# Delta over 64 rows in alternating partition halves; the weight's second half quantised in two 512-column chunks; M's third tile ahead of x G's fourth

## What is computed

```
delta = lora_B @ lora_A * 32/64                   # rank 64, 512 x 512
idx   = searchsorted(thresholds, (weight + delta) / exp(scale_log), side='left')   # 8 levels, 7 cuts
w_eff = codebook[idx] * exp(scale_log) + delta    # by groups of 128 columns
q, k, v = split((x @ w_eff.T) @ Wqkv + bqkv)
x = x + softmax(q k.T / sqrt(128)) v @ Wo + bo
y = x @ W.T + 2 * sum_e gate_e * (x A_e.T) B_e.T  # gates: softmax of the two best of 8 logits
x = x + y @ (scale * (qweight - zero_point)).T + bias
```

## Time and profile before

| | |
|---|---|
| device time, median of 3 runs | 107.92 us (107.66 to 108.25) |
| device time of the profiled execution | 108.04 us |
| span of its profile | 106.2 us |
| TensorE (PE) busy | 101.5 us, 96% |
| VectorE (DVE) busy | 66.3 us, 62% |
| ScalarE (ACT) busy | 51.9 us, 49% |
| GpSimd (POOL) busy | 34.3 us, 32% |
| mean granted TensorE clock | 0.997 |

### The profile page before, as it was taken

One profiled execution on the slowest core, in us unless ns is written; L12 is line 12 of the kernel. 1 busy time (PEld: TensorE's weight loads), 2 busy tenths in 40 slices (PEclk: granted clock), 3 DMA queues, 4 the chain that ended last, 5 costly groups with the idle time before them and its releaser, 6 DMA issues.

```text
span 106.2 us, 1428 instructions
## 1 busy us (share of the span) xinstructions
PE 101.5 (96%) x505; PEld 83.6 (79%) x505; DVE 66.3 (62%) x157; ACT 51.9 (49%) x92; POOL 34.3 (32%) x34
## 2 busy tenths in 40 slices
PE   6899999999999999999999999999999999999980
PEld 6734588889777899899888787889898888888850
DVE  1196799999999899325999653014946802572440
ACT  4038789999999954734222238272038204002000
POOL 3000063799919993696000056400000400000000
PEclk9999999999999999999999999999999999999998
DMA  1999999960000000000000000000000540000072
GB/s 38 323 259 396 408 402 406 408 244 0 3 0 0 0 0 0 9 0 0 0 0 0 0 0 0 0 6 0 0 0 0 225 170 0 6 0 0 0 294 104
DMA packets 4455, 9.83 MB, mean 93 GB/s; under 512 B 736, under 2 KB 736, under 8 KB 4448
## 3 DMA queue, kind: packets, MB, share of 16 engines
q1 hardware_dynamic: 4304, 9.48, 24.3%
q10 hardware_dynamic: 144, 0.26, 0.8%
HBM read 7.64 MB, written 2.10 MB: 92 GB/s over the span
## 4 chain that ended last, share of the span: by engine, by line
PE 89%; DMA 4%; DVE 3%; ACT 1%; issue 0%
PE psum L860 19%; PE psum L862 19%; PE psum L861 19%; PE psum L884 7%; PE psum L876 4%; DMA lora<-in_lora 4%; PE psum L895 3%; PE psum L910 3%; PE psum L901 3%; PE psum L905 3%; PE psum L1011 2%; PE psum L1032 2%; PE psum L1026 2%; ACT moe L459 1%; PE psum L1018 1%; PE psum L928 1%
## 5 line engine op out<-in xcount | busy, mean ns | idle before, releaser
L665 DVE COPY_PREDICATED cond_work<-cond_work,psum 128x1024 f32<-128x1024 int32 x10 | 13.7, 1374 | 1.3 <-ACT cond_work L359 0.9
L860 PE MATMUL psum<-G_hi,xT_hi 128*128 128x512 f32 x32 | 12.9, 402 | 0.0
L861 PE MATMUL psum<-G_lo,xT_hi 128*128 128x512 f32 x32 | 12.5, 391 | 0.0
L862 PE MATMUL psum<-G_hi,xT_lo 128*128 128x512 f32 x32 | 12.5, 390 | 0.0
L578 POOL TENSOR_TENSOR hl<-hl,hl_bias 128x272 f32<-128x272 f32 (+2 forms) x4 | 3.1, 774 | 27.0 <-ACT hl L370 14.3
L359 ACT ACTIVATE cond_work<-cond_n,cut_bias 128x1024 f32<-128x1024 f32 x10 | 11.4, 1158 | 0.7 <-DVE cond_n L704 0.7
L520 POOL TENSOR_TENSOR xT_lo<-xT,xT_hi 128x1024 fp32r<-128x1024 f32 x4 | 9.6, 2402 | 2.4 <-DVE cond_work L671 2.4
L860 PE MATMUL psum<-xT_hi,split_b_hi 128*128 128x512 f32 x24 | 9.7, 402 | 0.0
L862 PE MATMUL psum<-xT_hi,split_b_lo 128*128 128x512 f32 x24 | 9.4, 391 | 0.0
L861 PE MATMUL psum<-xT_lo,split_b_hi 128*128 128x512 f32 x24 | 9.4, 390 | 0.0
L520 POOL TENSOR_TENSOR split_a_lo<-moe,split_a_hi 128x512 fp32r<-128x512 f32 x3 | 4.3, 1436 | 15.0 <-ACT split_a_hi L336 12.5
(11 more groups left out here) (168 smaller groups left out, 239.8 us busy)
## 6 DMA issues: line engine op xcount, KB each, us to landing
out<-cond_work SPq DMA_DIRECT2D x8, 256.0 KB, 2.1
q_i<-in_q_t SPq DMA_DIRECT2D x4, 256.0 KB, 7.5
moe<-in_moe_w SPq DMA_DIRECT2D x4, 256.0 KB, 7.5
cond_n<-in_cond_w SPq DMA_DIRECT2D x2, 512.0 KB, 7.1
xT<-in_x_t SPq DMA_DIRECT2D x2, 512.0 KB, 8.2
xT<-in_x_t SPq DMA_DIRECT2D x1, 1024.0 KB, 12.7
wqkv_n<-in_wqkv SPq DMA_DIRECT2D x1, 768.0 KB, 10.7
hlT<-in_hl_t SPq DMA_DIRECT2D x1, 272.0 KB, 6.7
```

What stands on the lines that cost most here:

```text
L665: dve.copy_predicated(by_group(half(level, h)), by_group(beyond[n % len(beyond)].bitcast(I32)), psum[EARLY][:, at:at + GROUPS // 2].unsque ...
L860: pe.matmul(out_ap, l_hi, r_hi, start=first, stop=False)
L861: pe.matmul(out_ap, l_hi, r_lo, start=False, stop=False)
L862: return pe.matmul(out_ap, l_lo, r_hi, start=False, stop=last)
```

## The change

The diff has seven parts.

- Delta: each product takes 64 of the 128 partitions, the lower half for o = 0, 2 and the upper for o = 1, 3; the scale is no longer halved.
- `w_full(0)` moves ahead of VectorE's last small operations on the cuts.
- The rounding of moe tile 1 moves from ScalarE to GpSimd, with a semaphore of its own.
- `CHUNKS`: the quantisation runs in three chunks: tiles 0 and 1 (1024 columns), tile 2, tile 3 (512 columns each). 21 masks and picks take the place of 14. VectorE's and ScalarE's lists are laid out anew from the second chunk on.
- PE: the four `M_part(2, i)` come before `y_x(3)`, only the four `M_part(3, i)` behind it.
- PE: `y_o(0)` comes ahead of `scores(1, 0)`.
- The last result is added and stored in two column halves.

```diff
-    LORA_COPIES = 2
-    LORA_SCALE = 32.0 / 64.0 / LORA_COPIES
+    LORA_SCALE = 32.0 / 64.0
+    CHUNKS = (slice(0, 2), slice(2, 3), slice(3, 4))
...
-            for b in range(BATCH):
+            for b in range(BATCH - 1):
                 sp.wait_ge(y_ready, b + 1)
                 sp.dma_start(out[b], y_out[:, b, :]).then_inc(stored, 16)
+            b = BATCH - 1
+            for n in range(2):
+                sp.wait_ge(y_ready, b + n + 1)
+                s = slice(n * C // 2, (n + 1) * C // 2)
+                sp.dma_start(out[b, :, s], y_out[:, b, s]).then_inc(stored, 16)
...
             beyond_cut(0, 0)
-            moe_hi(1)
             w_hi(1)
...
             beyond_cut(0, 1)
+            beyond_cut(1, 1)
             hl_raw(1, 5)
-            beyond_cut(1, 1)
+            beyond_cut(2, 1)
...
             hl_raw(2, 6, HL)
-            beyond_cut(2, 1)
             x_hi(1)
...
             w_eff_hi(1)
             beyond_cut(3, 1)
+            beyond_cut(4, 1)
+            beyond_cut(5, 1)
             wqkv_round(1)
-            beyond_cut(4, 1)
+            beyond_cut(6, 1)
+            beyond_cut(0, 2)
+            beyond_cut(1, 2)
             wqkv_round(2)
+            beyond_cut(2, 2)
+            w_eff_hi(2)
             wqkv_round(3)
-            beyond_cut(5, 1)
-            beyond_cut(6, 1)
+            for j in range(3, CUTS):
+                beyond_cut(j, 2)
             act.wait_ge(loaded["woT"], 16)
             rounded(woT_hi, woT[:, :, :], woT_hi_ready)
-            w_eff_hi(2)
             w_eff_hi(3)
...
+            pool.wait_ge(loaded["moe1"], 16)
+            pool.tensor_copy(split_a_hi[:, 1, :], moe[:, 1, :]).then_inc(moe_first_hi_ready, 1)
             moe_rest(1)
...
+            w_full(0)
             dve.wait_ge(dve_step, cuts_at)
             keep(1, ALU.min, 3)
...
             for i in range(CT):
                 G_rest(i)
-            pick(0, 1)
-            pick(1, 1)
+            for j in range(3):
+                pick(j, 1)
             w_eff(0)
             w_eff(1)
...
-            pick(2, 1)
-            pick(3, 1)
-            pick(4, 1)
-            pick(5, 1)
-            pick(6, 1)
+            for j in range(3, CUTS):
+                pick(j, 1)
+            pick(0, 2)
             w_eff(2)
+            pick(1, 2)
+            w_eff_lo(2)
+            for j in range(2, CUTS):
+                pick(j, 2)
             w_eff(3)
-            w_eff_lo(2)
             w_eff_lo(3)
...
             for o in range(CT):
-                pe.matmul(psum[DELTA_BANKS[o]][:, :], lora[:, 0, o * P:(o + 1) * P], lora[:, 1, :], start=True, stop=True)\
+                rows = slice(o % 2 * RANK, (o % 2 + 1) * RANK)
+                pe.matmul(psum[DELTA_BANKS[o]][:, :], lora[rows, 0, o * P:(o + 1) * P], lora[rows, 1, :],
+                          start=True, stop=True)\
                   .then_inc(delta_done, 1)
...
-            pe.wait_ge(picked, HALVES * CUTS)
+            pe.wait_ge(wqkv_ready, 3)
+            pe.wait_ge(w_eff_late_lo_ready, 1)
+            for i in range(CT):
+                M_part(2, i)
+            pe.wait_ge(picked, len(CHUNKS) * CUTS)
             y_x(3)
             pe.wait_ge(wqkv_ready, CT)
+            pe.wait_ge(w_eff_late_lo_ready, 2)
             for i in range(CT):
-                for o in range(2, CT):
-                    pe.wait_ge(w_eff_late_lo_ready, o - 1)
-                    mm = M_part(o, i)
-                mm.then_inc(M_done, 1)
+                M_part(3, i).then_inc(M_done, 1)
...
+            pe.wait_ge(oT_hi_ready, 1)
+            pe.wait_ge(oT_lo_ready, 1)
+            y_o(0)
             pe.wait_ge(qkvT_ready, 6)
             scores(1, 0)
-            pe.wait_ge(oT_hi_ready, 1)
-            pe.wait_ge(oT_lo_ready, 1)
-            for t in range(TPH):
+            for t in range(1, TPH):
                 y_o(t)
```

More of the change, by code:

```diff
@@ L308, in _, with chunk, groups, beyond_of @@
             load("lang", lang_i[:, :], lang.partition_broadcast(P))
-            for b in range(BATCH):
+            for b in range(BATCH - 1):
                 sp.wait_ge(y_ready, b + 1)
                 sp.dma_start(out[b], y_out[:, b, :]).then_inc(stored, 16)
-            sp.wait_ge(stored, 16 * BATCH)
+            b = BATCH - 1
[3 more added lines that the diff above has]
+                sp.dma_start(out[b, :, s], y_out[:, b, s]).then_inc(stored, 16)
+            sp.wait_ge(stored, 16 * (BATCH + 1))
+        def chunk(ap, k):
+            return ap[:, CHUNKS[k], :].rearrange("p t (g n) -> p (t g) n", n=P)
+        def groups(k):
+            return CT * (CHUNKS[k].stop - CHUNKS[k].start)
+        def beyond_of(n, k):
+            return beyond[n % len(beyond)].rearrange("p (g n) -> p g n", n=P)[:, 0:groups(k), :]
         def by_group(ap):
@@ L358, in beyond_cut @@
                     act.wait_ge(picked, n - len(beyond) + 1)
-                act.activation(beyond[n % len(beyond)], half(cond_n, h), ACT.Relu, bias=cut_bias[:, j:j + 1], scale=CUT_GAIN)\
+                act.activation(beyond_of(n, k), chunk(cond_n, k), ACT.Relu, bias=cut_bias[:, j:j + 1], scale=CUT_GAIN)\
                    .then_inc(beyond_ready, 1)
@@ L539, in moe_rest @@
             def moe_rest(o):
-                pool.wait_ge(moe_hi_ready, o)
+                if o == 1:
+                    pool.wait_ge(moe_first_hi_ready, 1)
+                else:
+                    pool.wait_ge(moe_hi_ready, o - 1)
                 rest(split_a_lo[:, o, :], moe[:, o, :], split_a_hi[:, o, :], moe_lo_ready)
+            pool.wait_ge(loaded["moe1"], 16)
+            pool.tensor_copy(split_a_hi[:, 1, :], moe[:, 1, :]).then_inc(moe_first_hi_ready, 1)
             moe_rest(1)
@@ L652, in w_delta_first, with pick @@
                 dve.tensor_tensor(cond_n[:, 0:2, :], cond_n[:, 0:2, :], delta[:, 0:2, :], ALU.add).then_inc(wd_ready, 1)
-            def pick(j, h):
-                n = nth(j, h)
+            def pick(j, k):
+                n = nth(j, k)
                 dve.wait_ge(beyond_ready, n + 1)
@@ L663, in pick @@
                     dve.wait_ge(picked, n)
[L664 to L667, removed]
+                at = GROUPS * j + CT * CHUNKS[k].start
+                dve.copy_predicated(chunk(level, k), beyond_of(n, k).bitcast(I32),
+                                    psum[EARLY][:, at:at + groups(k)].unsqueeze(2).to_broadcast(
+                                        [P, groups(k), P])).then_inc(picked, 1)
             def w_eff(o):
-                dve.wait_ge(picked, nth(CUTS - 1, o // 2) + 1)
+                dve.wait_ge(picked, nth(CUTS - 1, max(0, o - 1)) + 1)
                 dve.tensor_tensor(level[:, o, :], level[:, o, :], delta[:, o, :], ALU.add).then_inc(w_eff_ready, 1)
@@ L698, in _ @@
             dve.tensor_scalar(cut_bias[:, :], cuts[:, :], -CUT_GAIN, None, ALU.mult).then_inc(cut_bias_ready, 1)
-            w_full(0)
             w_delta_first()
@@ L852, in _ @@
             gh_lo(1, 0)
-            for t in range(TPH, BATCH):
+            for t in range(TPH, BATCH - 1):
                 y_store(t)
+            for n in range(2):
+                y_store(BATCH - 1, slice(n * C // 2, (n + 1) * C // 2))
         @block.tensor
@@ L897, in G_product @@
             def G_product(o):
-                pe.wait_ge(moe_hi_ready, o)
+                if o == 1:
+                    pe.wait_ge(moe_first_hi_ready, 1)
+                else:
+                    pe.wait_ge(moe_hi_ready, o - 1)
                 pe.wait_ge(w_hi_ready, o)
```

19 lines of the change are left out of this document (10 added, 9 removed).

## The result

The changed kernel takes 109.69 us in the median of four runs (108.93, 109.04, 110.33, 110.53), the kernel before 107.88. The ratio is 1.0156, with a 95% interval of 1.0124 to 1.0189: slower by some 1.7 us, where 0.7 us less was forecast. The four runs lie in two pairs, 1.4 us apart; that is part of what has to be explained.

What follows compares the result with a forecast made beforehand. TensorE, busy 96% of the span, was taken as the bound. Gains 0.30 + 0.13 + 0.12 + 0.20 = 0.75, less 0.05 for small waits, made 0.70: forecast 107.2 us, range 106.7 to 107.8.

Steps and rivals of the forecast that it cites:

- All of it shifts by 0.30: Everything up to 30 us, TensorE included, follows w_lo(1) and comes 0.30 us earlier.
- zero gained, zero lost: New order of M with chunked picks: TensorE keeps 1.7 to 3.5 us spare, so no time changes.
- ScalarE's masks, halved too, stay ahead of VectorE: In the chunked quantisation, VectorE's picks never wait for ScalarE's masks.
- half pick: A pick of half the columns on VectorE: 0.69 us, starting 0.76 to 0.78 after the one before.
- Rival C: Half picks 1.05 us apart make VectorE's list late, y_x(3) waits 2.1 us: 109.3 us, chance 0.07.
- three signs of being wrong: w_lo(1) not moved, y_x(3) waiting for a pick, or the end after the last matmul not under 3.1 us.
- Delta: Early TensorE passes in halves pair up, five slots for eight, 1.29 us saved (bounds 0 and 1.72), held back by w_lo(1).
- Rival A: Delta's halves don't run side by side and the mode change costs a drain: 107.5 us, chance 0.13.
- w_lo(1): VectorE's operation before G's tile 1 ends 0.30 us earlier, at 14.90, as GpSimd's moe_rest(1) moves forward.
- Bf_lo: Comes about 0.4 us earlier through half picks, so TensorE no longer stops at y_x(0): 0.13 us gained.
- y_o(0): Placed before scores(1, 0) on TensorE, it removes the wait for the copy of q: 0.12 us gained.
- The end: Last addition and store in halves: 0.20 us gained, bounds -0.1 and 0.35.

Runs made afterwards that it cites:

- experiment 4: Changed kernel with GpSimd waiting for w_full(2) before moe_rest(2) and x's third pair earlier: 107.88 us; without chunks and M's new order, wait alone: 107.87 us.
- experiment 5: Kernel before with only delta in halves and w_full(0) forward: 107.99 us; experiment 4's kernel without chunks, woG_lo ahead of the bias rounding: 107.61 us.
- experiment 7: Moe's first tile back on ScalarE, no added GpSimd wait, woG_lo forward: without chunks 107.50 us; changed kernel so edited, x earlier too, 107.25 us.
- experiment 6: Kernel before with half stores 107.72, GpSimd wait 108.19, or moe cast on GpSimd 108.96 us; cured kernels, woG_lo forward, whole store: 107.78 (no chunks), 107.62 us.
- experiment 1: Changed kernel with GpSimd's moe_rest(2) made to wait until w_full(2) is done: 109.41 us, ratio 1.0139.

## Why the prediction was wrong, step by step

**The step that failed** is "All of it shifts by 0.30", with its twin for the chunks, "zero gained, zero lost". Both count slack between a producer and its consumer. For TensorE the second held: y_x(3) started at 45.18 without a wait, no product of M waited. The first did not: with 0.30 and 0.13 gained the end of M should have come 0.43 earlier, and the first product behind it starts at 50.05 instead of 49.28, 0.77 later. Neither step asked which operations would now meet on VectorE and GpSimd. What the runs showed in their place: w_full(2) beside moe_rest(2) takes 1.56 us instead of 0.54 and costs 1.0, the cast of lang beside GpSimd's x_lo takes 1.56 instead of 0.16 and costs 1.4. I had the rule in hand. The earlier trace rows show w_lo(1) waiting for GpSimd, and I used it to price a gain for that one operation, then moved GpSimd's and VectorE's lists against each other for 50 us as if it held nowhere else. The Trainium skill, GPSIMD Engine Reference, "Specifications", names instructions of VectorE with two SBUF inputs or in a 2-port mode as those that contend with GpSimd; VectorE: DVE Perf Modes, "Mode 2×_2P", gives that mode to single-source operations on SBUF. The traces agree: w_full(2) and the cast of lang have one data source in SBUF each, and waited, though no row shows the mode itself. I had read only the half of the rule that fitted w_lo.

**GpSimd's later transfers of work.** The prediction followed w_eff_lo(3) to TensorE, which had room (44.7 against 47.2), and not to GpSimd, whose woT_lo and both x_lo stand behind a wait for it. It also put w_eff_lo(3) at 44.7; it ended at 46.69. About 1.0 of that is the early collision. Most of the rest is a wait that the prediction had ruled out ("ScalarE's masks, halved too, stay ahead of VectorE"), on DVE:

```profile
33.81 0.76 DVE L689 COPY_PREDICATED cond_work<-cond_work,psum 128x512 f32<-128x512 int32 x1 [0.71 <-ACT cond_work L374]
```

ScalarE makes this mask from 33.07 on, behind the two roundings of w_eff. Every trace with chunks has this wait, 0.71 to 0.74. A half pick is also longer than forecast, 0.76 instead of 0.69, and starts 0.86 to 0.88 after the one before it instead of 0.77 (28.83, 29.71, 30.57 in the changed kernel). Rival C, the picks too slow, was near this in kind but had the wrong consumer: it priced a wait at y_x(3), which never came. No rival had VectorE and GpSimd meet, and none of the three signs of being wrong came: w_lo(1) had moved, y_x(3) didn't wait for a pick, and behind the end of the last matmul were 3.09 us, just under the 3.1 named.

**What lay around the span** was taken as it was, 1.84 us. It grew by 0.25.

**Term by term.** Delta: its passes ran side by side in pairs. PE and PEld of the changed kernel:

```profile
4.75 1.99 PE L904 MATMUL psum<-lora 64*128 64x512 f32 x8 [0.35 <-DMA lora<-in_lora]
4.72 0.33 PEld L904 LDWEIGHTS psum<-lora 64*128 64x128 f32 x4 [0.61 <-DMA lora<-in_lora]
5.26 0.22 PEld L904 LDWEIGHTS psum<-lora 64*128 64x128 f32 x2 [0.21 <-issue]
5.69 0.22 PEld L904 LDWEIGHTS psum<-lora 64*128 64x128 f32 x2 [0.21 <-issue]
15.18 1.19 PE L937 MATMUL psum<-split_b_lo,split_a_hi 128*128 128x512 f32 x4 [0.48 <-DVE split_b_lo L670]
```

The loads come two by two, 0.43 apart: eight passes in four slots, not the five that I took. G_first starts at 7.02 instead of 9.21, 2.19 earlier and so beyond the bound of 1.72, since in this profile the first passes too come at 0.43, where those of before took 1.82 for two. No drain shows ahead of G_first, which stands still for 0.28 and has w_full(0) named as its releaser; a drain shorter than that would be hidden. By the last row none of it reached the path, as forecast: TensorE waits for w_lo(1). Rival A is refuted.

w_lo(1): GpSimd's cast took 0.61 (0.52 forecast). From the addition on cond_n to its end are 5.93 us against 6.11, so 0.18 earlier, not 0.30; where cond_w0 lands early, as in experiment 4, only 0.07, because moe's tile then lands 0.56 earlier where the addition starts 0.67 earlier. In spans, moe on GpSimd is worth 0.28 (0.62 below before in experiment 5, 0.33 without it in experiment 7), and it costs 0.39 over the span with its wait. The sum's largest term was a loss.

Bf_lo: forecast 0.13, from "about 0.4 earlier" where the sum's own figures (30.2 against 27.89 + 2.88) give 0.6; the stall is gone, and with chunks the spans are 0.14 (experiment 6) and 0.15 (experiment 7) below those without, 0.05 in experiment 4. y_o(0): forecast 0.12; from the load of scores(0, 3) to the last matmul are 42.22 us against 42.36, so 0.14. The end: forecast 0.20, by a sum with a slip in it (a window of 0.8 that shrinks to 0.35 or 0.4 gives 0.40 to 0.45, not 0.35). From the start of the last matmul to the end of the span (106.239 and 108.223 us to three places) are 3.55 us in the kernel before and 3.49 in the changed one, and all other traces agree: 3.54 to 3.55 with a whole store, 3.49 to 3.50 with half stores. In means of spans, half stores alone gave 0.19 and, between experiments 5 and 6, 0.12. The traces show less than the runs do, and the interval of the ratio for that edit alone reaches past 1.

**The sum again.** From 107.9: less 0.45 in the span, plus 0.25 over it, plus the late collision of 1.4, is 109.1 for the pair at 109.0; the early collision's 1.0 on top gives 110.1 for the pair at 110.4. The 0.3 that are left are within what the landing of cond_w0 does to a run, but weren't tested. The two pairs I put down to w_full(2) meeting moe_rest(2) in some executions and not in others. That is argued, not shown: no run of a faster group was profiled. For it speaks that none of the kernels of experiments 1, 4, 5 and 6 that have the wait ahead of moe_rest(2) falls into two groups; in the traces with the collision the two start within 0.08 us of each other.

## What to carry to other kernels

Before moving work of VectorE or GpSimd, lay the two timelines over one another and mark every pair that comes to overlap; an operation that costs 0.16 alone can cost the rest of whatever GpSimd is doing. Follow each changed time to all its waiters, through the lists of the engines that have slack too, since an idle engine that starts late can sit on the one that has none. And compare the whole time with the span: a gain in the trace can be lost outside it.

## What the runs showed of the hardware

- VectorE's tensor_scalar and cast from and to SBUF wait out a GpSimd operation that starts with them or is under way: 1.54 to 1.65 us instead of 0.54, 1.39 to 1.56 instead of 0.16. The first ends 0.27 to 0.29 us after GpSimd's, the second 0.02 to 0.03. A w_full(2) that had started 0.32 us ahead of GpSimd's (before) kept its 0.54. A pick (128x1024, copy_predicated with its values in PSUM) beside the same GpSimd operation kept its 1.37.
- Two fp32 products of 64 rows in opposite partition halves run as pairs of passes, four slots of 0.43 us for eight passes in the changed kernel. In experiment 1 the pairs were 0.86 apart, half that pace, though the granted clock of the stretch reads 1.00 in both traces.
- One more wait on GpSimd's list, which held it by some 0.3 us, lengthened an execution by 0.25 us outside the span (twelve runs, 1.99 to 2.09 over the span, against 1.75 to 1.85 on the same chip). The cause is open.
- Splitting the last 256 KB store in two of 128 KB shortened the time after the last matmul by 0.05 us in the traces (3.54 to 3.55 against 3.49 to 3.50 us from its start).
